# A graph network's mesh product: three rounded products in place of a plain float32 one

## The reference, cut to what matters

```python
e = _mlp(mesh2grid_efeat, emb_W0, emb_b0, emb_W1, emb_b1, emb_g, emb_b)
...
e_in = jnp.concatenate([e, mesh_nfeat[src], grid_nfeat[dst]], axis=-1)
e_new = _mlp(e_in, edge_W0, edge_b0, edge_W1, edge_b1, edge_g, edge_beta) + e
```

## Time and profile before

| | us |
|---|---|
| median of three runs | 2294.68 |
| lowest and highest | 2293.87, 2297.41 |
| the profiled execution | 2294.92 |
| its span, first to last instruction | 2293.2 |
| mean granted TensorE clock, share of full | 0.985 |

### The profile page before, as it was taken

How to read it: one execution, slowest core, us unless ns; L and a number is a source line. 1 busy time by engine, 2 the same in 40 slices (tenths; PEclk the granted TensorE clock), 3 DMA queues, 4 the chain that set the end, 5 groups by cost and what they waited for, 6 DMA issues and landing times. The chain is left out here.

```text
span 2293.2 us, 44871 instructions
## 1 busy us (share of the span) xinstructions
PE 2192.8 (96%) x13036; PEld 1881.2 (82%) x13040; DVE 1502.4 (66%) x3372; ACT 1217.4 (53%) x2244; POOL 1209.9 (53%) x1721
## 2 busy tenths in 40 slices
PE   2989998999999999999999999999999999999898
PEld 2437886878778989989889898998989989889776
DVE  4813996353846776766766767667676676766666
ACT  1122113242337667666676766676676667667421
POOL 0387107786415555555555555555555555555223
PEclk7999999999999999999999999999999999999899
DMA  8232001010266323333332333333233333333131
GB/s 217 74 78 49 1 0 43 3 44 3 60 199 169 65 61 63 64 59 64 62 65 60 61 65 62 64 64 61 62 59 65 63 64 64 62 59 66 26 95 45
DMA packets 81519, 149.80 MB, mean 65 GB/s; under 512 B 20229, under 2 KB 20695, under 8 KB 81460
## 3 DMA queue, kind: packets, MB, share of 16 engines
q0 software_dynamic: 47248, 93.38, 21.4%
q1 hardware_dynamic: 34212, 55.67, 8.0%
HBM read 128.90 MB, written 19.71 MB: 65 GB/s over the span
## 5 line engine op out<-in xcount | busy, mean ns | idle before, releaser
L1654 ACT ACTIVATE b_bank<-c_bias 128x512 f32<-128x512 f32 x528 | 315.9, 598 | 15.1 <-PE b_bank L1766 5.2
L145 POOL DMA_INDIRECT s_attrs<-k_attrs,k_row_i x170 | 225.4, 1326 | 165.7 <-POOLq L2220 114.9
L1587 DVE CUSTOM_DVE_ANT_0 b_bank<-b_bank,c_p,k_floor 128x512 f32<-128x512 f32 x176 | 132.5, 753 | 255.7 <-PE b_bank L1788 254.8
L1432 POOL DMA_INDIRECT c_from_src<-s_dst_table,c_at_nodes x173 | 278.6, 1610 | 32.0 <-issue 32.0
L1843 PE MATMUL b_bank<-k_m_hi,c_pt_hi 128*128 128x512 f32 x704 | 293.8, 417 | 0.0
L1419 POOL DMA_INDIRECT c_from_src<-s_mesh_table,c_at_nodes x176 | 202.2, 1149 | 152.3 <-POOL c_at_nodes L1415 144.2
L1844 PE MATMUL b_bank<-k_m_lo,c_pt_hi 128*128 128x512 f32 x704 | 277.9, 395 | 0.0
L1845 PE MATMUL b_bank<-k_m_hi,c_pt_lo 128*128 128x512 f32 x704 | 274.0, 389 | 0.0
L1438 POOL TENSOR_TENSOR c_dev<-c_var,k_half 128x1 f32<-128x1 f32 x176 | 99.7, 566 | 327.1 <-DVE c_var L1569 327.1
L1725 ACT ACTIVATE c_h<-c_from_src 128x512 f32<-128x512 f32 x176 | 111.2, 632 | 263.3 <-DVE c_from_src L1608 263.3
L1786 PE MATMUL b_bank<-c_m_hi,c_ht_hi 128*128 128x384 f32 x704 | 222.5, 316 | 6.3 <-DVE c_ht_lo L1574 6.0
(11 more groups left out here) (352 smaller groups left out, 5859.8 us busy)
## 6 DMA issues: line engine op xcount, KB each, us to landing
k_w<-in_L_gnn_Ws_self_dram SPq DMA_DIRECT2D x3, 1024.0 KB, 6.8
k_w<-in_L_gnn_Ws_neigh_dram SPq DMA_DIRECT2D x3, 1024.0 KB, 10.8
c_from_src<-s_mesh_table,c_at_nodes POOLq DMA_INDIRECT x176, 3.5
c_from_src<-s_dst_table,c_at_nodes POOLq DMA_INDIRECT x173, 4.7
s_attrs<-k_attrs,k_row_i POOLq DMA_INDIRECT x170, 2.6
a_mesh<-in_L_gnn_mesh_nfeat_dram SPq DMA_DIRECT2D x10, 224.0 KB
k_h<-in_x_dram SPq DMA_DIRECT2D x1, 2240.0 KB
s_mesh_table<-a_mesh_out SPq DMA_DIRECT2D x10, 224.0 KB
```

Of the source, the lines that this page charges most:

```text
L145: return pool.indirect_dma_start(scratch["attrs"], bass.IndirectOffsetOnAxis(ap=k["row_i"][0:EP, c:c + 1], axis=0), k["attrs"][0:EP, A4 * ...
L1432: pool.indirect_dma_start(from_src[u][:], None, scratch["dst_head" if head else "dst_table"], bass.IndirectOffsetOnAxis(ap=at_nodes[u][:, ...
L1587: dve.tensor_tensor_reduce(var1_bank[:], var1_bank[:], p[u % 2][:], 1.0 / D, k["floor"][:, 0:1], ALU.mult, ALU.add, var[u][:, 0:1]).then_i ...
L1654: act.activation(bank[:], bias[:, m, :], ACT.Copy).then_inc(bank_set, 1)
```

## The change

The mesh product takes the layer's form. `w0b` is split once: ScalarE writes its high part into the place of `w0a` behind the second row result, and VectorE writes its low part over `w0b` itself. `mesh_t` becomes a rounded tensor, which ScalarE writes as before. For each block VectorE subtracts it from the transposed block in the bank (`mesh_low`) into `mesh_lo`, two buffers in the place of `wnb`. TensorE waits for the low part and makes `product` over four chunks, twelve float32r matmuls where four float32 ones stood. On VectorE the low parts of blocks 0 and 1 stand ahead of their result copies; in the loop the low parts of both blocks of a pair stand ahead of the pair's result copies. The `w_lo` subtractions keep their place ahead of the loop.

```diff
--- before.py
+++ after.py
@@ -118,6 +118,7 @@
 
 
 SORT_AT, TEMP_AT, FOLD_AT, SBUF_END = 87296, 112128, 132864, 229344
+W0A_AT, WNB_AT, W0B_AT = (FOLD_AT + n * KC * D * 4 for n in (6, 7, 8))
 SUMS_AT, LATE_AT, AGG_AT, U_AT, SPARE_AT = 24768, 90624, 104192, 179968, 220928
 
 
@@ -219,12 +220,17 @@
     w1t = [fd(f"w1t_{i}", [P, KC, D]) for i in range(2)]
     w1gt = [fd(f"w1gt_{i}", [P, KC, D]) for i in range(2)]
     w0a, wnb, w0b = (fd(n, [P, KC, D]) for n in ("w0a", "wnb", "w0b"))
+    assert fold.at == W0B_AT + KC * D * 4
     jobs_out = [fd(f"jobs_out{i}", [P, D]) for i in range(2)]
     rows_out = [fd(f"rows_out{i}", [3, D]) for i in range(2)]
     mesh = [fd(f"mesh{i}", [NPB, D]) for i in range(2)]
-    mesh_t = [fd(f"mesh_t{i}", [P, KC, P]) for i in range(2)]
+    mesh_t = [fd(f"mesh_t{i}", [P, KC, P], F32R) for i in range(2)]
     mesh_out = [fd(f"mesh_out{i}", [NPB, D]) for i in range(2)]
 
+    w0b_hi = Region(nc, W0A_AT, SBUF_END)("a_w0b_hi", [P, KC, D], F32R)
+    w0b_lo = Region(nc, W0B_AT, SBUF_END)("a_w0b_lo", [P, KC, D], F32R)
+    late_low = Region(nc, WNB_AT, SBUF_END)
+    mesh_lo = [late_low(f"a_mesh_lo{i}", [P, KC, P], F32R) for i in range(2)]
     h, w = keep["h"], [keep["w0"], keep["w1"]]
     w_hi, w_lo, hc, ht_hi, ht_lo = ([keep[f"{n}{i}"] for i in range(2)] for n in ("w_hi", "w_lo", "hc", "ht_hi", "ht_lo"))
     bias0, u_hi, u_lo = keep["bias0"], keep["u_hi"], keep["u_lo"]
@@ -254,6 +260,7 @@
     mesh_in = [sem(f"mesh_in{i}") for i in range(2)]
     mesh_stored = [sem(f"mesh_stored{i}") for i in range(2)]
     mesh_turned, mesh_t_ok, mesh_mm, mesh_ok = (sem(n) for n in ("mesh_turned", "mesh_t_ok", "mesh_mm", "mesh_ok"))
+    w0b_hi_ok, w0b_ok, mesh_lo_ok = sem("w0b_hi_ok"), sem("w0b_ok"), sem("mesh_lo_ok")
     hot_ok = sem("hot_ok")
     count_mm = [sem(f"count_mm{b}") for b in range(3)]
     copied_out = [sem(f"copied_out{b}") for b in range(3)]
@@ -564,12 +571,25 @@
             dve.wait_ge(mesh_mm, n + 1)
             dve.tensor_copy(mesh_out[u][:], bank[6 + u][0:NPB, :]).then_inc(mesh_ok, 1)
 
+        def mesh_low(n, u, fixed):
+            dve.wait_ge(mesh_t_ok, n + 1)
+            if not fixed:
+                dve.wait_ge(mesh_mm, n - 1)
+            dve.tensor_tensor(mesh_lo[u][:, :, 0:NPB], spread(bank[4 + u]), mesh_t[u][:, :, 0:NPB].bitcast(F32),
+                              ALU.subtract).then_inc(mesh_lo_ok, 1)
+
+        dve.wait_ge(w0b_hi_ok, 1)
+        dve.tensor_tensor(w0b_lo[:], w0b[:], w0b_hi[:].bitcast(F32), ALU.subtract).then_inc(w0b_ok, 1)
+        for u in range(2):
+            mesh_low(u, u, True)
         for u in range(2):
             mesh_copy(u, u, True)
         for i in range(2):
             dve.wait_ge(w_hi_ok, i + 1)
             dve.tensor_tensor(w_lo[i][:], w[i][:], w_hi[i][:].bitcast(F32), ALU.subtract).then_inc(w_lo_ok, 1)
         with dve.Fori(1, NB // 2) as i:
+            for u in range(2):
+                mesh_low(2 * i + u, u, False)
             for u in range(2):
                 mesh_copy(2 * i + u, u, False)
 
@@ -657,6 +677,8 @@
             act.wait_ge(job_out[r % 2], rows_stored(r % 2, r))
             m = len(vectors[r][0])
             act.activation(rows_out[r % 2][0:m, :], bank[r % 2][0:m, :], ACT.Copy).then_inc(row_out_ok, 1)
+            if r == 1:
+                act.activation(w0b_hi[:], w0b[:], ACT.Copy).then_inc(w0b_hi_ok, 1)
 
         act.wait_ge(next_in, MOVED + 32)
         for i in range(2):
@@ -771,18 +793,20 @@
         def turn(n, u, fixed):
             pe.wait_ge(mesh_in[u], MOVED if fixed else (n - u) * (MOVED // 2) + MOVED)
             if not fixed:
-                pe.wait_ge(mesh_t_ok, n - 1)
+                pe.wait_ge(mesh_lo_ok, n - 1)
             for c in range(KC):
                 last = pe.transpose(bank[4 + u][:, c * P:c * P + NPB], mesh[u][:, c * P:(c + 1) * P], k["ident"][0:NPB, 0:NPB])
             last.then_inc(mesh_turned, 1)
 
         def multiply(n, u, fixed):
-            pe.wait_ge(mesh_t_ok, n + 1)
-            if not fixed:
+            pe.wait_ge(mesh_lo_ok, n + 1)
+            if fixed:
+                pe.wait_ge(w0b_ok, 1)
+            else:
                 pe.wait_ge(mesh_ok, n - 1)
-            for c in range(KC):
-                last = pe.matmul(bank[6 + u][0:NPB, :], mesh_t[u][:, c, 0:NPB], w0b[:, c, :], start=(c == 0), stop=(c == KC - 1))
-            last.then_inc(mesh_mm, 1)
+            left = (lambda c: mesh_t[u][:, c, 0:NPB], lambda c: mesh_lo[u][:, c, 0:NPB])
+            product(pe, bank[6 + u][0:NPB, :], left, (lambda c: w0b_hi[:, c, :], lambda c: w0b_lo[:, c, :]),
+                    range(KC)).then_inc(mesh_mm, 1)
 
         for u in range(2):
             turn(u, u, True)
```

## The result

The changed kernel takes 2298.41 us (median of 22 runs), the kernel before, run beside it, 2294.98 (22 runs as well): 3.4 us more, ratio 1.0016, interval 1.0010 to 1.0023. The forecast was 2297.4 against 2294.68, 2.7 more, within 0.2%; by the medians it is 0.15%, with an interval that reaches a little over 0.2%.

The account below looks back on a forecast made before the run. TensorE, busy for 96% of the span, was taken as the bound. First pair 1.06 us earlier, second leaving 4.45 late, 1.68 regained: 2.76 late; 2294.92 + 2.76, less 0.24, gave 2297.4 us, range 2293.2 to 2300.8.

Parts of the forecast that it names:

- Part 1: Mesh products: 24 rounded products take 5.69 us where a pair's plain float32 ones took 6.97, a gain of 1.28.
- Part 2: VectorE's subtraction before the products: 0.72 us more per pair, so an undisturbed pair takes 7.68 in place of 8.24.
- Part 3: Splitting w0b on ScalarE and VectorE: fits between row results and into VectorE's idle stretch, costs nothing.
- Part 4: First mesh pair: low clock for 4.65 us costs 2.11, products take 7.80, next transposes start 1.06 us earlier.
- Part 5: Second mesh pair: TensorE idle 4.93 us behind the weights' low parts on VectorE, half clock again; pair takes 13.75 us.
- Part 6: Last three mesh pairs and after: 1.68 us back, layer starts 2.76 us late, nothing later absorbs or doubles it.
- the two clock terms: First and second mesh pairs: low clock after the long wait, charged at 2.11 us in each.
- A: Second mesh pair runs at half clock to its end: 4.66 us, sum +5.3, total 2300.0; chance 0.14.
- B: No clock drop at the second mesh pair's wait: sum +0.65, total 2295.3; chance 0.15.
- C: Mesh rows load late, two pairs each losing 0.56 us at most: sum +3.9, total 2298.5; chance 0.07.
- D: Steady mesh pairs lose the clock during 1.99 us without products: 14 us more, total 2311.4; chance 0.02.
- E: VectorE's queue lets block 2's low part past the weights' low parts: sum -3.3, total 2291.4; chance 0.02.

Follow-up runs that it names:

- plain products: Changed kernel with one plain float32 matmul per chunk, of the high parts alone, products with low parts left out; 2304.83 us, ratio 1.0049.
- ScalarE's order: On top of both low parts early, ScalarE makes the first pair's mesh copies ahead of the weights' high parts and node copies; 2297.05 us, ratio 1.0008.
- both low parts early: Changed kernel with both low parts of the layer's weights moved ahead of the first pair's result copies on VectorE; 2291.66 us, ratio 0.9995.
- transposes moved: On top of both low parts early, a block's transposes placed behind the products of the block two before; 2294.58 us, ratio 1.0004.
- both: Changed kernel with both low parts early, ScalarE's order and transposes moved together; 2292.09 us, ratio 0.9988 to the kernel before.
- both, 12 scatters: Both low parts early, ScalarE's order and transposes moved, with 12 in place of 24 early GpSimd scatters; 2279.58 us, ratio 0.9940.

## Why the prediction was right

The direction, the place and the size held: 2297.4 with a range of 2293.2 to 2300.8, measured 2298.41. Step by step:

- **Part 1, passes.** 24 products take 5.70 (158.61 - 152.91), forecast 5.69. The row was the better guide: by the Trainium skill's figure (TensorE: Matmul & The Clock Gate, "Wait — 56ns, not 53.3ns?") it would have been an estimated 5.18. With plain products behind the same waits the pair takes 1.27 more, forecast 1.28.
- **Part 2, the new step.** 2.07 us from transposes to products, forecast 1.99; the pair 7.77, forecast 7.68. The row was one of straight code, and the mesh pairs are a loop. That the loop makes the difference is not shown: with ScalarE's order the first pair, straight code as well, took 2.04 (122.66 - 120.62). Over three pairs it is 0.27.
- **Part 3, the split of `w0b`.** No cost on either engine.
- **Part 4, the first pair.** Products start 6.57 behind the transposes, forecast 6.60. They took 8.36 in place of 7.80: the half clock lasted 5.8 us, not 4.65. This term was sized too low, by 0.56. The mean of four was a poor choice: only two of them, 5.3 and 5.4, follow a wait of about 5 us, and alone would charge 2.43 in place of 2.11. The stretch at 55.8 follows a wait of 29.32, and the one at 2174.2 is counted from its products, though TensorE had started again at 2171.70 with the clock at 0.50 already. But no single value is right either. With both low parts early, the first pair has the same code and the same wait of 5.49, and its products took 7.84, a half clock of some 4.7 us.
- **Part 5, the second pair.** The wait is 4.93 to the digit, 5.95 (142.78 - 136.83 = 5.95) from the transposes. The half clock lasted 5.2, again over 4.65, and the pair took 14.01, forecast 13.75. The experiments divide its loss: with both low parts early the pair takes 7.80, so 6.2 us hang on the queue order, of which 3.85 are waiting and 2.36 the clock.
- **Part 6, the sum.** 3.83 in the stage, forecast 2.76. The 1.1 between them are the two clock terms (0.8) and the loop's 0.08 (0.3). The total, 3.4 more in place of 2.7, hides part of this, and the layer's first transposes at 174.16, forecast 174.27, agree by luck: they hold the 1.18 by which this execution reached the stage earlier. The counting stage did not change (120.1), so nothing absorbed or doubled the delay, as forecast. That held only in this direction: of a start 5.1 us earlier than in the kernel before (both low parts early, 228.5 against 233.6) about 1 us was lost, and one 8.9 us earlier (transposes moved) was lost whole, which I had not looked for.

Of the rivals, A (half clock to the pair's end) did not come: the low stretch ended at 148. B did not: the clock fell. C did not: no transposes waited for rows in the changed kernel. D is refuted by a clock of 1.00 over the three steady pairs. The Trainium skill (TensorE: Matmul & The Clock Gate, "Part 4: PE-mode transpose") says that transposes do not count as busy the same way. The trace does not decide on this: even with them counted as idle, the steady pairs are only 2.07 us at a time without products, and no run here has transposes alone. E did not come either: the low part of block 2 starts at 142.06, behind the weights' low parts, and moves only when the order in the program does (both low parts early).

## What to carry to other kernels

When a change puts a new step of an engine on another's path, read what already stands in that engine's program ahead of the step: 4.5 us of work that cost nothing while only copies were queued behind it cost 6.2 once TensorE was, more than a third of it through the clock. A faster stage gives its gain only if the next one can start earlier; check what other queues, here GpSimd's scatters, still have to do at that earlier time, and move them too. A control that makes the same move in the kernel before tells whether the move has a price of its own.

## What the runs showed of the hardware that was not expected

- TensorE's issue slows to two or three matmuls every 0.73 us for 8 to 10 us when counting starts with many GpSimd scatters still to come. Counted at the start of counting, 10 scatters were still to start with ScalarE's order, 7 with transposes moved and 12 with both. With both low parts early (5), in the kernel before (2) and in "both, 12 scatters" (1) it did not happen, though in the first of these both engines were busy side by side for 8 us. It can end before the last scatter (234.5 and 237.4 with ScalarE's order). Taking scatters away removes it. By which path scatters hold up TensorE's issue stays open: no run separated the loading of code, the traffic of semaphores and the descriptors, and a change of the scatters' number moves all of them.
- After a wait of TensorE of 2.72 us, behind 1.0 us of transposes, the clock fell too, 0.4 to 0.6 us behind the restart of the products.
- The half clock after waits of about 5 us lasted 5.8 and 5.2 us of products in the changed kernel, some 4.7 in the first pair with both low parts early (behind 5.49), and some 3.4 in the second pair of plain products (behind 4.92). After the wait of 2.72 it was 3.4 as well. So its length does not follow from the wait, and a single value for it, as I took, is good to 1.4 us of stretch, 0.6 us of time.
